# GpSimd's row gathers in the first three edge stages of a four-layer GNN: what each group of four waits for

## The reference

```
h = relu(layernorm(x)); x = x + L0(h)   # Wr = Wh[row]; Wc = Wh[col]; weight = cosine(Wr, Wc) * ...; segment_sum(weight * Wc, row)
h = relu(layernorm(x)); x = x + L1(h)   # msg = relu(h[src] + edge_attr_32 @ We + be); segment_sum(msg, dst)
h = relu(layernorm(x)); x = x + L2(h)   # msg = mlp(concat(hn[src], mlp(edge_attr_64))); segment_sum(msg, dst)
h = relu(layernorm(x)); x = x + L3(h)   # attention over 6 heads, softmax by dst, segment_sum(alpha * gl[src], dst)
```

## Time and profile before

| | |
|---|---|
| device time, 3 runs | 4990.21 us median (4989.92 to 4996.32) |
| the profiled execution | span 5820.0 us from first to last instruction; no other time of that execution is recorded |
| busy over the span | PE 75%, DVE 71%, POOL 56%, PEld 49%, ACT 35% |
| mean granted clock of PE | 0.875 |
| gathers | 2830: 806 in edge0, 608 in edge1, 608 in edge2 (16 of them ahead of the stage), 808 in edge3a |

### The profile page before, as it was taken

One profiled execution on the slowest core, in us unless ns is written; L12 is line 12 of the kernel. 1 busy time (PEld: TensorE's weight loads), 2 busy tenths in 40 slices (PEclk: granted clock), 3 DMA queues, 4 the chain that ended last, 5 costly groups with the idle time before them and its releaser, 6 DMA issues. The chain is left out here.

```text
span 5820.0 us, 104938 instructions
## 1 busy us (share of the span) xinstructions
PE 4388.1 (75%) x29528; PEld 2834.6 (49%) x29528; DVE 4126.9 (71%) x7954; ACT 2011.5 (35%) x6556; POOL 3270.2 (56%) x2950
## 2 busy tenths in 40 slices
PE   2999899989677777756777777376777667549998
PEld 1444444444344444445555555244444434349998
DVE  4767676766777676767777777466666666789998
ACT  2656566666000000134434444000000000057775
POOL 4666666663566666455555554455555555325554
PEclk6999999999788888778888888688888888779998
DMA  4333333331212111121111111233333333211111
GB/s 114 91 90 94 87 87 93 94 87 48 52 43 44 40 43 44 23 47 45 45 42 47 44 45 35 63 101 103 100 103 101 105 106 102 78 43 47 49 49 33
DMA packets 493105, 394.00 MB, mean 68 GB/s; under 512 B 346007, under 2 KB 379168, under 8 KB 492904
## 3 DMA queue, kind: packets, MB, share of 16 engines
q1 hardware_dynamic: 395496, 303.53, 18.3%
q0 software_dynamic: 90560, 83.37, 8.0%
q10 hardware_dynamic: 6976, 6.23, 0.3%
HBM read 355.34 MB, written 37.42 MB: 67 GB/s over the span
## 5 line engine op out<-in xcount | busy, mean ns | idle before, releaser
L1093 POOL DMA_INDIRECT edge_src_rows<-table_wh,edge_gather_idx x806 | 867.8, 1077 | 503.0 <-issue 229.7
L950 POOL DMA_INDIRECT edge3a_src_rows<-table_h,edge3a_gather_idx x808 | 763.1, 944 | 632.7 <-issue 259.0
L2165 PE MATMUL edge3a_z_ps<-Wz,edge3a_both_ends_t 128*128 128x396 f32 x1616 | 736.3, 600 | 405.0 <-DVE edge3a_terms L2258 322.0
L1123 PE MATMUL edge_sums_ps<-edge_onehot_src,edge_halves 128*128 128x512 bf16 x4840 | 890.0, 331 | 43.2 <-issue 32.4
L950 POOL DMA_INDIRECT table_cat<-table_hn,table_gather_idx x592 | 624.9, 1056 | 479.6 <-PE edge_sums_ps L1795 181.2
L1508 POOL DMA_INDIRECT edge_src_rows<-table_h,edge_gather_idx x608 | 609.1, 1002 | 424.4 <-issue 175.4
L2258 DVE SCALAR_TENSOR_TENSOR edge3a_terms<-edge3a_z_ps,att_z 128x792 f32<-128x792 f32 x404 | 386.1, 977 | 486.6 <-DMA edge_edge_attr<-in_ea 307.5
L2165 PEld LDWEIGHTS edge3a_z_ps<-Wz,edge3a_both_ends_t 128*128 128x128 f32 x1616 | 346.6, 226 | 733.7 <-DVE edge3a_terms L2258 368.3
L1123 PEld LDWEIGHTS edge_sums_ps<-edge_onehot_src,edge_halves 128*128 128x128 f16 x4840 | 385.6, 97 | 477.4 <-issue 69.5
L2577 PE MATMUL edge3b_sums_ps<-edge3b_onehot,edge3b_weighted 128*128 128x128 f32 x4848 | 572.9, 279 | 6.3 <-DVE layers_accT L2615 4.4
L2577 PEld LDWEIGHTS edge3b_sums_ps<-edge3b_onehot,edge3b_weighted 128*128 128x128 f32 x4848 | 553.6, 193 | 12.0 <-DVE layers_accT L2615 4.6
(11 more groups left out here) (370 smaller groups left out, 7950.6 us busy)
## 6 DMA issues: line engine op xcount, KB each, us to landing
edge_dst_row<-in_dst_row SPq DMA_DIRECT2D x102, 512.0 KB
edge3a_dst_row<-in_dst_row SPq DMA_DIRECT2D x102, 512.0 KB
edge_window<-table_wh_parts SPq DMA_DIRECT2D x816, 48.8 KB
edge3a_window<-table_h SPq DMA_DIRECT2D x816, 32.0 KB
edge_edge_attr<-in_ea SPq DMA_DIRECT2D x101, 256.0 KB
kept_rows<-edge3a_src_rows SPq DMA_DIRECT2D x101, 256.0 KB
edge3b_src_rows<-kept_rows SPq DMA_DIRECT2D x101, 256.0 KB
edge_edge_attr<-in_ea SPq DMA_DIRECT2D x101, 128.0 KB
```

The source lines that it names most:

```text
L950: nc.gpsimd.indirect_dma_start(self.slot(b, j), None, self.table[:, :], bass.IndirectOffsetOnAxis(ap=self.idx[b][:, j:j + 1], axis=0)).the ...
L1093: nc.gpsimd.indirect_dma_start(g[q][:, j, :], None, k.t_wh[:, :], bass.IndirectOffsetOnAxis(ap=idx[q][:, j:j + 1], axis=0)).then_inc(gathe ...
L1123: mm = pe.matmul(acc[:, i, 0:w], halves[q][:, j, a, :, :].rearrange("p h d -> p (h d)"), hot[:, o:o + w], start=first and a == 0, stop=False)
L2165: mm = pe.matmul(zp[q % 2][:, i, 0:H * ZH], hcT[h][:, j * P:(j + 1) * P], k.Wz[:, :], start=True, stop=True)
```

## The change

In edge0, edge1 and edge2 every wait of the second kind is replaced. A group of four gathers now waits until the group before it has landed, wherever that one was: in the same batch for a group that starts at tile 4 (8, 12), in the batch or pair gathered before for a group that starts at tile 0. The waits that protect buffers and the wait for the indices stay. Edge3a keeps its own `midway`.

```
-                        if j % 4 == 0:
-                            wait_past(pool, used_v, NV * (t - 3) + j * NV // PB + 1)
+                        if j == 0:
+                            wait_past(pool, gathered[1 - q], 16 * PB * (m + q))
+                            pool.sem_inc(gate, 1)
+                        elif j % 4 == 0:
+                            pool.wait_ge(gathered[q], 16 * (PB * m + j))
                             pool.sem_inc(gate, 1)
...
-                                if j == 0 and p == 2:
-                                    wait_past(pool, sums_ready, GROUP * (gi - 1) + 3)
+                                if j == 0:
+                                    wait_past(pool, gathered[(p + 2) % TAKEN], 16 * B * (gi + (p > 0)))
                                     pool.sem_inc(gate, 1)
-                                if j == B // 2:
-                                    if p == 0:
-                                        wait_past(pool, sums_ready, GROUP * (gi - 1) + 1)
-                                    else:
-                                        wait_past(pool, m_ready, GROUP * (gi - 1) + p + 2)
+                                elif j == B // 2:
+                                    pool.wait_ge(gathered[p], 16 * (B * gi + j))
...
-                    if h == 1:
-                        if j == 0:
-                            wait_past(pool, rp_ready, GROUP * (m - 1) + 2)
-                        else:
-                            wait_past(pool, catTp_ready, GROUP * (m - 1) + 5)
-                    elif q == 0 and j:
-                        wait_past(pool, sums_ready, 2 * GROUP * (m - 1))
-                    elif q == 1 and j == 0:
-                        wait_past(pool, sums_ready, 2 * GROUP * (m - 1) + 4)
-                    elif q == 1:
-                        wait_past(pool, rp_ready, GROUP * (m - 1) + 4)
+                    b = 2 * q + h
+                    if j:
+                        pool.wait_ge(ga.gathered[b], 16 * (B * m + j))
+                    else:
+                        wait_past(pool, ga.gathered[(b + 2) % TAKEN], 16 * B * (m + (b > 0)))
```

## The result

The changed kernel takes 5755.07 us (5751.81 to 5759.39, 4 runs) against 4991.67 us (4989.92 to 4996.32, 4 runs) of the kernel before. The ratio is 1.153, 95% interval 1.1513 to 1.1546: 763 us slower. The forecast was 5530, with 5220 to 5800 as its range.

A forecast was written before the change was run, and what follows sets the result against it. POOL's rate of serving groups of four gathers was to bound edge0 and edge1. The +326 us on the profiled span became 279 us if scaled, or 799; the middle, +540 on 4990, gave 5530 us, range 5220 to 5800.

The forecast's parts named there:

- Landing gap: Between groups of four gathers on POOL: idle 2.2 us instead of 0.30, bounded by 1.58 and 2.64 us.
- POOL bounds the stages: Edge0 and edge1 run at POOL's rate, 7.42 and 7.12 us per group; edge2 just fits, 0 us; chance 0.80.
- From the profiled to the plain execution: Turns +326 us on the profiled span into plain time: 279 us or 799 us, middle taken, +540.
- second end: Plain stages shrink but gathers and landing do not: 364 + 286 + 149 = 799 us in edge0, edge1, edge2.
- What bounded the kernel before: PE sets edge0's pace; edge1 and edge2 are a chain between engines; nobody is kept by a gather.
- The queue behind: SP's later index loads, row loads and 16 windows behind waiting gathers in edge0: priced at nothing; uncovered, 17 us per stage.
- Landing hidden: Rival in the three stages: gap 1.58 us and gathers shrink with the rest, cost 91 us, 5080; chance 0.10.
- No change: Rival: groups with the landing fit the plain cadences, or POOL is far from the bound; 4990; chance 0.03.
- Faster: Rival: landing waits avoid collisions with VectorE that lengthen gathers in edge0, edge1 and edge2; 4943; chance 0.03.
- worse case: Rival: PE idles more in edge0 and its clock falls, to 0.70 another 166 us, 5955; above 5800, chance 0.04.

The follow-up runs named there:

- disturbed execution: The first profile of the unchanged kernel before, with a span of 5820 us, 830 us over its plain time; the source of the forecast's rows.
- undisturbed profile: The kernel before, unchanged, profiled once more: 4991.31 us with a span of 4989.5 us.
- edge0 alone: The new landing waits in edge0 only, edge1 and edge2 as in the kernel before: 5318.20 us, ratio 1.065.

## Why the prediction was right, and where its size was off

**Landing gap.** Taken as 2.2 us between 1.58 and 2.64. Measured 2.36, 2.28 and, in edge2, 321.8/147 = 2.19. The groups were put at 7.42, 7.12 and 7.33 us and came to 7.38, 7.19 and 7.24. This step carried the forecast and held within 2%, in edge0 with some luck: the gap was longer by 0.16 us than put in, and the four gathers shorter by 4 x (1.077 - 1.020) = 0.23. The lower bound was sound, since a matmul does start about 1.6 us after the last gather. The upper bound of 2.64 us came from the disturbed execution: undisturbed, edge3a has no gap over 0.4 us.

**POOL bounds the stages.** Right for all three: each alone costs what its group takes over the old cadence, the costs add up, and they follow the number of waits up and down.

**From the profiled to the plain execution.** This is the step that was mis-sized. The prediction had two ends, 279 us if all scales and 799 us if stages shrink and gathers do not, and took the middle, 540, for which it had no row. So 5755 lies in the range, but 225 us above the forecast and 45 below the upper end. Measured: 763 us, near the second end. The cadences of that end, 5.62, 5.24 and 6.32 us, meet the plain 5.64, 5.24 and 6.23 almost to the digit. The gathers are the same in the disturbed and the undisturbed execution: 944 and 946 ns at the mean in edge3a, 0.30 us between them. Two arguments had pulled the forecast down. That POOL would already be full in edge1 was taken to speak against the second end; it was simply true. That PE needs 5.8 us per group in edge0 came from the disturbed execution; busy 198.27 of 200 us at 5.64 us per group, PE needs 5.6.

**What remains between 799 and 763.** By the gathers, edge0 lasts 350 us longer, edge1 297 and edge2 149, together 796. From edge0's last gather to edge1's first, 102.3 us became 81.7, from edge1's to edge2's 113.1 became 117.9, and from edge2's to edge3a's 70.4 became 56.3: 30 us come back. For edge0 the reason can be read: DVE's last product started 33.2 us after the last gather before and starts 12.3 us after it now, because POOL no longer ends ahead of its users. 796 - 30 = 766.

**What bounded the kernel before.** The prediction called edge1 a chain between engines and said that nobody waits for gathers. In the undisturbed profile PE waits 145.7 us for them, and POOL is full. In edge0 it said that the old waits hold POOL back, by 222 us; undisturbed it is 31.9 us in 28 waits. Edge2 had no room of 7.38 us per group but 6.23, so it costs 137 us, not 0.

**The queue behind.** Pricing SP's index loads and windows at nothing held: in the profile of edge0 alone that stage's gathers take 342 us longer, 22 come back before edge1, and the span is 322 us longer than before, so nothing is left for SP.

**The rivals.** Landing hidden (5080) is out with a gap of 2.3 us. The Trainium skill, DMA: Bandwidth & Descriptors, section "Anatomy of one DMA — SWDGE (gpsimd) path", with some 2.0 us of fixed cost, led to 5.75 us for a group; the trace has 7.38 and 7.19. From the last gather's start to the next group's it is 0.94 + 2.28 = 3.2 us in edge1, of which 0.64 is the restart seen above. No change is out. Faster was tested by taking all spacing away: gathers in edge0 were shorter by 30 ns, and the time stayed. In the changed kernel they are shorter too, 1020 ns against 1060, 991 against 1007 and 1025 against 1064, some 65 us of POOL's time in all, and the change costs 763 us all the same. What makes some gathers long goes with VectorE's work: of the 214 gathers of the undisturbed edge0 that last over 1 us, 201 overlap the one-hot TENSOR_SCALAR of L1211, of the 592 shorter ones 294 do, and in edge3a, where no gather is over 962 ns, VectorE runs none. This agrees with the exclusion that the Trainium skill, SBUF — State Buffer, section "Who interferes with whom", states for VectorE's two-port modes; that this instruction runs in such a mode no row shows. PE's clock did fall, as the worse case had it, from a granted 1.00 to 0.91 in edge0:

```profile
600.00:800.00 200.00, 169.66 (x1166) 82.80 (x1188) 125.89 (x260) 113.20 (x104) 110.77 (x109) 0.91 0.34 79
```

PE's 169.66 busy us of 200 still leave room, so it cost nothing. PE's busy share went from 0.99 to 0.85 and not from 0.91 towards 0.80, because the 0.91 was of the disturbed execution.

## What to carry to other kernels

A wait for the landing of the very transfer issued last puts the whole latency, here 2.3 us in place of 0.30, between two issues; no buffer hides it, because it lowers the rate and not the lead. The same wait one group later was free here. Before pricing an added wait, compare the issuing engine's serial time per group with the stage's cadence, and take that cadence from a profile whose span agrees with the plain time. A stage whose gaps on that engine are all at the 0.30 us of plain issue is full, whatever its busy share says. In this case, where the profile was 17% over the plain time, the engine whose durations and gaps inside a group were untouched was the one to count at full price.

## What the runs showed of the hardware that was not expected

- One profiled execution was 830 us longer than another of the same kernel (5820.0 against 4989.5). DVE, ACT and POOL were busy as long in both to within 11 us, PE some 290 us longer (4388.1 against 4096.6, with 175 of its records missing in the second) at a granted clock of 0.875 against 0.906; which of it is cause and which effect is open. The four stages with gathers were longer by 16 to 31% (edge1 931 us against 796, edge3a 1325 against 1009), while edge3a's gathers stayed at 944 to 946 ns and edge3b at 5.98 us per batch in both.
- A gather on POOL that starts after a wait comes 0.64 to 0.73 us later than a matmul on PE that waits for the same landing (51 pairs in edge1; 2144.88 and 2144.24 is one).
- The gap did not shrink with fewer transfers under way: 2.34 us after two gathers, 2.28 after four, 2.30 after eight (172.3/75) in edge1.
